# A four-layer graph network on one core: the second layer's neighbour sums with their table cut into products of 512, 384 and 256 columns

## The reference

```python
h = jnp.maximum(_layernorm(x, axis=-1), 0.0)
x = x + layer(h, adj, weights)
```

```python
h_gat = jax.nn.relu(_layernorm(h_gat, gat_g, gat_b))
h_agg = jnp.einsum('mn,bnh->bmh', A_final, h_gat)
h_gin = (1.0 + eps) * h_gat + h_agg
z = jnp.einsum('bmh,hk->bmk', h_gin, W1) + b1
```

## Time and profile before

| | us |
|---|---|
| median of 3 runs | 1016.21 (1014.95 to 1017.24) |
| span of the profiled execution | 1013.8 |
| PE busy | 949.6 (94%) |
| PEld busy | 902.1 (89%) |
| DVE busy | 859.2 (85%) |
| ACT busy | 632.5 (62%) |
| POOL busy | 555.4 (55%) |
| mean granted TensorE clock | 0.980 |

### The profile page before, as it was taken

The page is one execution under the profiler, slowest core; times in us unless marked ns, Lnnn a source line. Parts: engine busy times, 40 slices in busy tenths (PEclk is TensorE's granted clock), DMA queues, the critical chain, the costliest instruction groups (busy, mean ns, idle before and its releaser), DMA issues. The chain is left out here.

```text
span 1013.8 us, 21212 instructions
## 1 busy us (share of the span) xinstructions
PE 949.6 (94%) x7355; PEld 902.1 (89%) x7355; DVE 859.2 (85%) x2526; ACT 632.5 (62%) x1655; POOL 555.4 (55%) x1171
## 2 busy tenths in 40 slices
PE   5989999999999999999999999998999999997998
PEld 4779998988998889899989899998999898886897
DVE  5988897989979988977888888799988989779874
ACT  3347547686668653775686664877548584677741
POOL 3535264582575652765566565654636744467850
PEclk9978999999999999999999999999999999999999
DMA  5020000000020010011000101101000100000003
GB/s 135 1 63 1 1 2 1 2 1 1 2 83 2 1 43 2 1 37 49 2 1 2 43 1 43 43 2 33 11 1 2 42 2 2 21 1 2 1 1 105
DMA packets 38071, 19.99 MB, mean 20 GB/s; under 512 B 3142, under 2 KB 37452, under 8 KB 37964
## 3 DMA queue, kind: packets, MB, share of 16 engines
q1 hardware_dynamic: 36080, 18.42, 6.5%
q10 hardware_dynamic: 1884, 0.21, 0.2%
HBM read 10.23 MB, written 8.39 MB: 18 GB/s over the span
## 5 line engine op out<-in xcount | busy, mean ns | idle before, releaser
L686 PE MATMUL ps<-HE,PT 128*128 128x129 f32 x2048 | 238.5, 276 | 3.2 <-issue 1.9
L686 PEld LDWEIGHTS ps<-HE,PT 128*128 128x128 f32 x2048 | 233.1, 192 | 5.4 <-issue 4.8
L451 ACT ACTIVATE Y<-X,SM 128x128 f32<-128x128 f32 x512 | 204.0, 491 | 49.3 <-POOL SM L447 49.1
L1307 DVE SCALAR_TENSOR_TENSOR PT<-ps,CE,maskT 128x512 f32<-128x512 f32 x256 | 174.2, 742 | 19.2 <-PE ps L810 11.8
L432 POOL TENSOR_TENSOR SM<-ST 128x8 f32<-128x8 f32 x96 | 29.5, 307 | 269.4 <-DVE ST L1170 269.3
L443 POOL TENSOR_TENSOR SM<-SM,minus_half 128x8 f32<-128x8 f32 x96 | 163.3, 1701 | 7.6
L686 PE MATMUL ps<-W,HT 128*128 128x128 f32 (+1 forms) x768 | 126.1, 311 | 0.0
L686 PEld LDWEIGHTS ps<-W,HT 128*128 128x128 f32 x768 | 115.6, 193 | 8.9
L1170 DVE BATCH_NORM_STATS2 ST<-X 128x6 f32<-128x128 f32 x512 | 104.8, 278 | 3.1 <-DMA X<-in_x_dram 0.4
L703 PE MATMUL ps<-ident,Y 128*128 128x128 f32 x640 | 85.6, 278 | 10.7 <-ACT Y L451 10.2
L703 PEld LDWEIGHTS ps<-ident,Y 128*128 128x128 f32 x640 | 72.2, 143 | 16.3 <-ACT Y L451 14.4
(11 more groups left out here) (260 smaller groups left out, 2335.6 us busy)
## 6 DMA issues: line engine op xcount, KB each, us to landing
X<-in_x_dram SPq DMA_DIRECT2D x32, 256.0 KB, 3.5
out_dram<-X SPq DMA_DIRECT2D x32, 256.0 KB, 2.8
adj_raw<-in_adj_dram SPq DMA_DIRECT2D x4, 256.0 KB, 3.5
W<-in_L_gnn_W_dram SPq DMA_DIRECT2D x2, 64.0 KB, 3.8
W<-in_L_gnn_W_dram SPq DMA_DIRECT2D x1, 128.0 KB, 3.6
bias<-in_L_gnn_bias_dram SPq DMA_DIRECT2D x2, 64.0 KB, 4.1
Wo<-L_gnn_others_weight_dram ACTq DMA_DIRECT2D x1, 64.0 KB, 3.1
feat1w<-in_L_gnn_Wp_dram ACTq DMA_DIRECT2D x1, 64.0 KB, 3.5
```

Of the source, the lines that this page charges most:

```text
L451: a = nc.scalar.activation(dst[:, n, 0:F], src[:, n, 0:F], func, scale=SM[s][:, S_RSTD, n:n + 1], bias=SM[s][:, S_SHIFT, n:n + 1])
L686: return nc.tensor.matmul(o, w, m, start=start, stop=stop, skip_group_check=True)
L1307: a = V.scalar_tensor_tensor(out=PT[r][:, j, :], in0=o, scalar=CE[s][:, c:c + 1], in1=maskT[:, j, :].bitcast(F32), op0=ALU.max, op1=ALU.mult)
```

## The change

The two tables become one, gin, with six blocks of 128 columns for each row block j. Four are the blocks of the high table, at places 0, 2, 3 and 5; the rest of the diagonal block takes place 1 (for j = 0 and 1) or 4 (for j = 2 and 3), beside or two places away from the others. The low-part product reads the four high blocks at places 0, 2, 3, 5, again 512 columns. The two products on HI cover five blocks between them: one of 384 columns takes the low block and two high blocks at equal distance (places 1,2,3 or 1,3,5 or 0,2,4 or 2,3,4) and writes three adjoining blocks of the tile; the other takes the remaining two high blocks, 256 columns, and writes them to their places, which for j = 0 and 3 are the first and last quarter of the tile. The sums are the same, in another order. In the setup ACT's one copy becomes four of 512 columns; DVE's copies change only their places. The order of work is not touched.

```diff
-        gin_hi = sb("gin_hi", [P, T, N], F32R)
-        gin_lo = sb("gin_lo", [P, T, P], F32R)
+        gin = sb("gin", [P, T, 6, P], F32R)
...
+        GIN_AT = (0, 2, 3, 5)
+        GIN_LOW = (1, 1, 4, 4)
+        GIN_THREE = ((1, 1, 0), (1, 2, 1), (0, 2, 0), (2, 1, 1))
+        GIN_PAIR = ((0, 5, 0, 3), (0, 2, 0, 1), (3, 2, 2, 1), (0, 5, 0, 3))
+
+        def gin_high(j):
+
+            return gin[:, j, :, :].rearrange("p (a c) n -> p a c n", a=2)[:, :, 0:3:2, :]
...
-                A(gin_hi[:], maskT[:].bitcast(F32), ACT.Copy).then_inc(made["gin_hi"], 1)
+                for k in range(T):
+                    a = A(gin_high(k), maskT[:, k, :].bitcast(F32).rearrange("p (a c n) -> p a c n", a=2, c=2), ACT.Copy)
+                a.then_inc(made["gin_hi"], 1)
...
-                    a = V.tensor_copy(gin_hi[:, k, k * P:(k + 1) * P], diagg[:, k, :])
+                    a = V.tensor_copy(gin[:, k, GIN_AT[k], :], diagg[:, k, :])
                 link(a)
                 for k in range(T):
-                    V.tensor_tensor(gin_lo[:, k, :], diagg[:, k, :], gin_hi[:, k, k * P:(k + 1) * P].bitcast(F32),
+                    V.tensor_tensor(gin[:, k, GIN_LOW[k], :], diagg[:, k, :], gin[:, k, GIN_AT[k], :].bitcast(F32),
                                     ALU.subtract)
...
                         for j in range(T):
-                            for m in (LO, HI):
-                                MM(o, m[s][:, j * G + b, :], gin_hi[:, j, :], j == 0 and m is LO, False)
-                            mm = MM(o[:, j * P:(j + 1) * P], HI[s][:, j * G + b, :], gin_lo[:, j, :], False, j == T - 1)
+                            r = j * G + b
+                            o4 = o.rearrange("p (c n) -> p c n", n=P)
+                            MM(o4.rearrange("p (a c) n -> p a c n", a=2), LO[s][:, r, :], gin_high(j), j == 0, False)
+                            at, step, to = GIN_THREE[j]
+                            MM(o4[:, to:to + 3, :], HI[s][:, r, :], gin[:, j, at:at + 2 * step + 1:step, :], False, False)
+                            at, step, to, apart = GIN_PAIR[j]
+                            mm = MM(o4[:, to:to + apart + 1:apart, :], HI[s][:, r, :],
+                                    gin[:, j, at:at + step + 1:step, :], False, j == T - 1)
                         mm.then_inc(done, 1)
```

## The result

| | before | changed |
|---|---|---|
| median of 20 runs, us | 1014.96 (1012.29 to 1019.93) | 1017.12 (1012.77 to 1024.06) |
| ratio to before, 95% interval | | 1.0030 (1.0016 to 1.0043) |
| span of the profiled execution, us | 1013.8 | 1015.4 |
| PE busy, us | 949.6 | 947.7 |
| mean granted TensorE clock of that execution | 0.980 | 0.975 |

The account below looks back on a forecast made before the run. The bound was taken as shared, PE leading, with chains through DVE, ACT and POOL. Of 6.4 us less PE work, 3.0 was to reach the end: span 1013.8 to 1010.8, plus 2.4 around it, 1013.2 us; range 1009.8 to 1016.6.

Parts of the forecast that it names:

- The price of the products: Second layer's neighbour sums (gin1): each period of three products falls from 0.577 to 0.526 us, 6.5 us over 128.
- the middle taken for 384 columns: New 384-column product in gin1: priced at 0.175 us, the middle between 0.119 (256 columns) and 0.232 (512).
- The gaps: Reading and writing in pieces of 128 columns in gin1's products: priced at 0, bound 0 to 5 us.
- The setup: ACT's one copy becomes four: nothing to 0.7 us more, hidden by rank's first copy waiting 0.74 us for PE.
- How much reaches the end: Of PE's 6.4 us less work over 16 groups, 7.5 groups x 0.40 = 3.0 us shorten the span.
- The walk: Path traced back from the end over engine timelines: PE holds 570 of 985 us, six groups wholly on it.
- the contested ones: Twelfth and fourteenth groups: page's chain and walk disagree on whether PE leads; one of them counted in the 7.5.
- It is absorbed: Rival: other paths tied with PE's cut each saving at the next join; half of 2.4 us left, 1014.9 us; 0.23.
- The one on the slow side: Rival: each jump between pieces in gin1's products restarts the stream, 35 us more work, 1036 us; chance 0.08.

Follow-up runs that it names:

- table_only: New six-block table, four setup copies and new places, but the products as in the kernel before; ratio to before 0.9994, 1014.02 us.
- pair of filled profiles: 49 useless 512-column products at eleven places where PE waits, added to the kernel before (1013.50 us) and to the changed kernel (1010.14 us).
- pad_after: Changed kernel plus one extra 512-column product at the head of each of the 32 gin1 tiles; 1014.90 us, ratio to before 0.9996.
- no_low: Changed kernel without three of the four low-part products of each gin1 tile; 1018.47 us, ratio to before 1.0036.
- fill_first: Changed kernel plus six 512-column products ahead of the first tile of the first group's gin1; 1016.30 us, ratio to before 1.0014.
- before2: The kernel before run again with no edit, for a second profile; 1013.00 us, ratio to before 0.9996.
- after2: The changed kernel run again with no edit, for a second profile; 1019.08 us, ratio to before 1.0034.

## Why the prediction was wrong

**The price of the products: right.** The period was to be 0.526 us and is 0.525; the middle taken for 384 columns held (344 ns with some of it at the lower clock, about 340 forecast), the pair lasts 286 ns (280).

**The gaps: right.** Pieces cost nothing. The rule of the Trainium skill that I had weighed against the trace (PSUM — Partial Sum Buffer, Specifications (TRN2), any non-contiguous pattern slows matmuls significantly) isn't borne out here for pieces of 128 columns. The period is 0.525 us for row block j = 0, whose pair writes the first and last quarter of the tile, and 0.525 for j = 1 and 2, whose pairs write adjoining blocks; and table_only shows that reading in pieces costs nothing.

**The setup: right.** The four copies last 716 ns each, and ACT's first copy of rank still waits for PE, 0.47 us where it was 0.74. table_only shows no cost.

**How much reaches the end: mis-sized.** The term was 7.5 groups x 0.40 = 3.0 us; the pair of filled profiles shows 1.3 us. The walk named six groups as wholly on the path. The second brings 0.58 us, the seventh 0.37, the tenth and eleventh together 0.47; the fourth and sixth bring nothing, nor do the contested ones. So the step that failed here is the walk: it took each group on the path for a full 0.40 us at the end. What the walk can't show is how close the other side was. PE's wait behind the fifth group, for ACT, was 0.36 us before; in the changed kernel the same wait and a new one behind the sixth group read:

```profile
306.43 1.14 PE L820 MATMUL ps<-ident,CE 128*128 128x128 f32 x8 [0.75 <-ACT HE L1011]
...
418.45 0.50 PE L696 MATMUL ps<-bias,pick 128*128 128x512 f32 x1 [0.28 <-DVE MX L1302]
```

0.36 became 0.75: the group's 0.40 us turned into idle time right behind it. And 0.28 us appeared where there had been no wait. The walk followed PE through the sixth group because PE had no gap there, but no gap is not slack on the other side. From the start of that group's gin1 to this product PE takes 8.00 us before (408.76 to 416.76) and 7.98 in the changed kernel (410.47 to 418.45): DVE's result came just when PE asked for it, and there was nothing to win. That the other path is within one saving of PE's in many places would also explain why work added costs half and work removed next to nothing; this is argued, not tested.

**What the sum had no term for: the clock.** I read a granted clock of 1.00 in the step and priced the saving there, and held the rest of the clock as given, though the profile of before already stood at 0.980, which is (1 - 0.980) / 0.5 x 1013.8 = 41 us at half speed. The changed kernel's profile has (1 - 0.975) / 0.5 x 1015.4 = 51 us. Most of the saving turns into longer idle times of PE, more falls of the clock come with them, and one of these costs 1 to 2.5 us of the path, as much as three to six groups save. That is how a change that takes 6.5 us of work away loses 3. That the lower clock comes from the shorter gin1 is shown for the sum, by pad_after, no_low and the filled kernels; fill_first adds the fall near 150 in one profile. For that fall the longer wait is the likely cause: it is absent behind waits of 1.52 to 1.63 us (before, before2, table_only, pad_after) and present behind 1.76 (both profiles of the changed kernel) and 2.48 (no_low). For the others a longer wait doesn't explain it. Near 310 us both profiles of the changed kernel have waits of 0.75 or 0.77 and of 1.34 us, and the clock falls in one of them only. Near 600 the wait ahead of the fall is 0.43 us, where it was 0.44 before without a fall. In after2 the fall at 216 follows a wait of 1.33 us that before, before2 and the first profile of the changed kernel have too, without a fall. So a fall can come or stay away behind one and the same wait. A rival is left: that any shift of the schedule can bring or remove a fall. pad_after and the fillings, which shift it too, don't exclude it. The Trainium skill tells of such a mechanism (TensorE: Matmul & The Clock Gate, HAM oscillation — how this bites in real kernels): a wait between bursts of products makes the gate close, and the next burst starts at the lower clock. This case's trace agrees in part. Near 309 us in the changed kernel the clock fell during the wait of 1.34 us, and the product behind it took 0.77 us where it took 0.47. Near 150 the products behind the wait of 1.76 us began at the upper clock, and the fall came about 1 us later.

**The rivals.** "It is absorbed" (0.23) was the nearest, and its arithmetic, half of 2.4 us, is what the filled pair shows. The one on the slow side had the wrong mechanism. Nothing in the prediction had the clock move. A rival of "the saving lengthens a wait that PE already has, and the clock falls" could have been worked out from the row of the 1.63 us wait, which lies in the middle of the step that the change shortens.

**Open.** The change's own worth at an equal clock lies between about 0 (lines through the runs of the unfilled kernels) and 3.4 us (medians of the filled pair, with a part from the clock). What decides whether the clock falls behind a given wait is open, and so is which of the eleven places of filling matter.

## What to carry to other kernels

On a TensorE that is 94% busy beside an engine that is nearly as loaded, a saving on TensorE alone is worth what the slack of the other paths allows; look at each wait near the edited step for who comes second, not only for who comes last. Read the mean granted clock of every run beside its time: a change that takes work from TensorE beside its waits can cost more through the clock than it saves, and products without use, placed where the engine waits anyway, are a cheap test and here a gain of 0.3 to 0.5%.

## What the runs showed of the hardware that I had not expected

The mean granted clock differs from run to run of one kernel (0.969 to 0.983 for the kernel before), and with it the time, by 0.5 to 0.7 us for 0.001. That is the spread of the times here: before's runs at 0.983 have a mean of 1012.8 us, those at 0.975 one of 1017.2. The clock can fall with PE at work: in the changed kernel it fell about 1 us after the wait of 1.76 us had ended and stayed low through 7 us in which PE's records show no pause. That wait differs by little between the kernels, 1.63 and 1.76 us, with 0.2 us less work on either side, and the fall is in both profiles of the one and in none of the other; two profiles of each are no more than a hint. Behind other waits the fall comes and goes with none of the work changed: the kernel before has falls near 475 and 520 us in one profile and near 820 and 920 in the other.
